# The output gate in one ScalarE function, in a delta-rule attention and mixture-of-experts kernel on one core

## The reference

```
o = scan over time of S = a S + k (v - k S) b;  o_t = q S
o = o * rsqrt(mean(o^2) + eps) * norm_w
o = o * (z * sigmoid(z))             # the gate
out = o @ out_w.T;  x = x + out
...then per token: router, top 2 of 8 experts, relu(x W1) W2, weighted sum
```

## Time and profile before

| | |
|---|---|
| median of 3 runs | 1410.39 us (1410.18 to 1411.52) |
| profiled execution, its own time | 1407.17 us |
| its span | 1405.3 us |
| granted TensorE clock, mean | 0.933 |
| chain that ended last, by engine | DVE 32%, PE 26%, POOL 16%, issue 10%, DMA 7%, ACT 6% |

### The profile page before, as it was taken

One profiled execution on the slowest core, in us unless ns is written; L12 is line 12 of the kernel. 1 busy time (PEld: TensorE's weight loads), 2 busy tenths in 40 slices (PEclk: granted clock), 3 DMA queues, 4 the chain that ended last, 5 costly groups with the idle time before them and its releaser, 6 DMA issues.

```text
span 1405.3 us, 33741 instructions
## 1 busy us (share of the span) xinstructions
PE 1172.5 (83%) x11978; PEld 944.4 (67%) x11978; DVE 1167.0 (83%) x2531; ACT 834.4 (59%) x2536; POOL 710.7 (51%) x598
## 2 busy tenths in 40 slices
PE   0355989898989899898989899999898988469992
PEld 0233868686868686777777777777777777358881
DVE  6878898988888889888888889898989894578875
ACT  1242666665666666666666656566665655348884
POOL 3151726465545555564646373828291914235552
PEclk9996999998989999999999999999999999789996
DMA  6031212222122222222212131313030314332225
GB/s 206 0 98 31 73 36 71 57 59 61 54 62 53 62 54 62 54 61 54 63 52 66 49 69 47 83 35 97 21 99 21 105 18 134 95 105 74 79 64 180
DMA packets 163174, 97.07 MB, mean 69 GB/s; under 512 B 115623, under 2 KB 148269, under 8 KB 161988
## 3 DMA queue, kind: packets, MB, share of 16 engines
q1 hardware_dynamic: 124932, 82.25, 21.5%
q10 hardware_dynamic: 33536, 4.20, 2.1%
q0 software_dynamic: 4544, 8.47, 1.9%
HBM read 73.31 MB, written 24.61 MB: 70 GB/s over the span
## 4 chain that ended last, share of the span: by engine, by line
DVE 32%; PE 26%; POOL 16%; issue 10%; DMA 7%; ACT 6%; SPq 2%; POOLq 0%; DVEq 0%; ACTq 0%
POOL kq L637 9%; DVE Y_sb L1056 7%; DVE blkT L1060 7%; PE kx L1541 3%; POOL decay L629 3%; POOL rows_in L609 2%; DMA blkN<-scr_n 2%; PE kx L1636 2%; POOL kq L620 2%; PE rc L1703 2%; DVE blkN L1047 2%; DVE Gs L1204 1%; DVE area L1146 1%; ACT Gs L836 1%; PE rc L1704 1%
## 5 line engine op out<-in xcount | busy, mean ns | idle before, releaser
L637 POOL TENSOR_TENSOR kq<-tapA,area 128x256 f32<-128x256 f32 x256 | 253.2, 1003 | 89.1 <-DVE area L1146 88.1
L758 ACT ACTIVATE area<-pj,taps 128x256 f32<-128x256 f32 x256 | 123.3, 482 | 138.8 <-PE pj L1555 130.4
L1056 DVE TENSOR_TENSOR Y_sb<-blkT,blkN 128x4 f32<-128x4 f32 (+18 forms) x304 | 172.4, 567 | 10.5
L1541 PE MATMUL kx<-kq 128*128 128x128 f32 x1024 | 143.1, 288 | 43.2 <-ACT area L767 32.6
L609 POOL DMA_INDIRECT rows_in<-rowbuf,dest x64 | 64.8, 1012 | 214.8 <-DVE dest L1132 187.3
L1541 PEld LDWEIGHTS kx<-kq 128*128 128x128 f32 x1024 | 130.2, 199 | 57.8 <-issue 41.2
L1143 DVE SCALAR_TENSOR_TENSOR tapA<-pj,taps,tapA 128x256 f32<-128x256 f32 x256 | 122.2, 477 | 51.7 <-ACT tapA L758 49.8
L620 POOL TENSOR_TENSOR kq<-kq,area 128x1024 f32<-128x1024 f32 x64 | 151.1, 2363 | 0.0
L1060 DVE TENSOR_REDUCE blkT<-Y_sb 128x2 f32<-128x4 f32 (+18 forms) x304 | 142.5, 469 | 5.2
L758 ACT ACTIVATE tapA<-pj,taps 128x256 f32<-128x256 f32 x256 | 123.1, 481 | 0.0
L1146 DVE SCALAR_TENSOR_TENSOR area<-pj,taps,area 128x256 f32<-128x256 f32 x256 | 121.4, 474 | 0.0
(11 more groups left out here) (305 smaller groups left out, 3593.6 us busy)
## 6 DMA issues: line engine op xcount, KB each, us to landing
area<-scr_alpha SPq DMA_DIRECT2D x32, 512.0 KB, 4.2
area<-scr_acum SPq DMA_DIRECT2D x32, 512.0 KB, 3.8
blkN<-scr_n SPq DMA_DIRECT2D x32, 256.0 KB, 4.3
area<-rows_in SPq DMA_DIRECT2D x39, 130.0 KB, 2.2
scr_n<-area SPq DMA_DIRECT2D x128, 32.0 KB, 1.6
area<-rows_out SPq DMA_DIRECT2D x4, 1024.0 KB, 8.0
rows_in<-rows_in SPq DMA_DIRECT2D x8, 260.0 KB, 3.8
kq<-in_x SPq DMA_DIRECT2D x4, 512.0 KB, 6.0
```

What stands on the lines that cost most here:

```text
L637: nc.gpsimd.tensor_tensor(dst[:, n % H, :], tapA[:, n % RING, :], tapB[:, n % RING, :], ALU.add).then_inc(conv_done, 1)
L758: ins = nc.scalar.activation(dst[:, n % RING, :], pj[n % 2][:, k:k + GT], ACT.Copy, scale=taps[:, t, k:k + 1])
L1056: ins = nc.vector.tensor_tensor(p4, bc(blkT[:, r0:, j:].rearrange("p r (o m) -> p r o m", o=1), [128, nr, w, wd]), bc(blkN[:, j:j + w, j:] ...
L1541: ins = mm(o, lhs[:, hh, cs], rhs_[:, hh, cs], start=True, stop=True)
```

## The change

The step `zt` of ScalarE applies Silu instead of Tanh, with scale 1/64 instead of 0.5/64, and raises `zg_ready` itself. The VectorE step `zg` is no longer there (the words `zg.c.u` stay in `ORDER` and issue nothing). ScalarE waits for `g_ready` of the group being finished before it overwrites `zg`. The output weights are scaled by norm_w / 256 only. The semaphore `z_tanh` is gone; the first count of `zg_ready` is given by ScalarE.

```diff
@@ ScalarE, before the first stage
-            for t in (z_tanh, kd_ready, rhs_ready, u_ready, sq_done, gn_ready, gt_ready):
+            for t in (zg_ready, kd_ready, rhs_ready, u_ready, sq_done, gn_ready, gt_ready):
                 act.sem_inc(t, HALVES)
@@ ScalarE, prepare, step "zt"
                         c, u = arg
+                        if g is not None:
+                            act.wait_ge(g_ready, halves(g, c, u))
                         act.wait_ge(z_mm, halves(a, c, u))
-                        nc.scalar.activation(zg[:, c, HU * u:HU * u + HU, :], heads(pj[u]), ACT.Tanh,
-                                             scale=0.5 / WSCALE).then_inc(z_tanh, 1)
+                        nc.scalar.activation(zg[:, c, HU * u:HU * u + HU, :], heads(pj[u]), ACT.Silu,
+                                             scale=1.0 / WSCALE).then_inc(zg_ready, 1)
@@ VectorE, before the first stage
-            nc.vector.tensor_scalar(ow[:, :, :], ow[:, :, :], nw[:, 0:1], 0.5 / WSCALE / VSCALE, ALU.mult,
+            nc.vector.tensor_scalar(ow[:, :, :], ow[:, :, :], nw[:, 0:1], 1.0 / VSCALE, ALU.mult,
                                     ALU.mult).then_inc(s_wsplit, 1)
...
-            for t in (n_ready, at_ready, zg_ready, S_ready, g_ready):
+            for t in (n_ready, at_ready, S_ready, g_ready):
                 dve.sem_inc(t, HALVES)
@@ VectorE, prepare
-                    elif step == "zg":
-
-                        c, u = arg
-                        dve.wait_ge(z_tanh, halves(a, c, u))
-                        nc.vector.scalar_tensor_tensor(out=half(zg, c, u), in0=half(zg, c, u), scalar=1.0,
-                                                       in1=heads(pj[u]), op0=ALU.add, op1=ALU.mult).then_inc(zg_ready, 1)
```

More of the change, by code:

```diff
@@ L197, in preln_delta_moe_kernel @@
         (diag_ready, decay_done, kk_ready, n_ready, ktr_ready, kd_ready, scale_ready, kq_ready, at_ready,
-         ka_ready, aq_ready, z_mm, z_tanh, zg_ready) = sems(
+         ka_ready, aq_ready, z_mm, zg_ready) = sems(
             "diag_ready decay_done kk_ready n_ready ktr_ready kd_ready scale_ready kq_ready at_ready ka_ready "
-            "aq_ready z_mm z_tanh zg_ready")
+            "aq_ready z_mm zg_ready")
         (blk_in, inv_step, inv_done, t_out, t_in, rdiag) = sems("blk_in inv_step inv_done t_out t_in rdiag")
```

## The result

| | before | after |
|---|---|---|
| median of all runs, same chip | 1410.18 us | 1416.12 us |
| lowest and highest of 13 runs | 1405.44, 1413.25 | 1412.64, 1421.15 |
| profiled execution, its span | 1407.17, 1405.3 us | 1415.49, 1413.6 us |
| mean granted clock of TensorE | 0.933 | 0.926 |
| periods of L490, 13 of them from the third tick on | 890.10 us | 893.82 us |

The ratio is 1.0047, 95% interval 1.0031 to 1.0063: the changed kernel is slower by half a per cent. The forecast was 0.7% faster, and 1416 lies above its range.

The account below looks back on a forecast made before the run. No engine full; the stage's chain of waits bounds it, VectorE handing to POOL at the seam. -9.8 (13 stages) - 0.5 (start) + 0.6 (tables) = -9.7 us: profiled 1407.17 to 1397.5, median 1400.5 us, range 1391 to 1410.

Parts of the forecast that it names:

- What bounds the kernel, and the hand-over to POOL: Seam of two stages: VectorE's gate steps stand directly before its hand-over to POOL; the scatter would start 1.19 us earlier.
- 13 stages at 0.75 us: Stages with a scatter: POOL's earlier start would save 0.75 us each, bounds 0 and 1.21; 9.8 us in all.
- The quiet stage: Period before the first scatter, 67.05 us, 1.21 less than the mean of twelve; taken as measure of POOL's lead.
- rival A: Seam of two stages: held by the DRAM round trip alone, so only 0 to 3 us gained, 1409 us; chance 0.17.
- the first pair: Gate steps `zg.0.0`, `zg.0.1` ahead of `ps`: without them the scatter and POOL's head of the next stage start 1.19 us earlier.
- The second pair at nothing: Gate steps behind `ps`, ahead of `at` and `st`: costed at nothing, as ScalarE and the round trip hold the first tap.
- The rule that I had cited as neutral: VectorE instructions with two SBUF inputs and GpSimd's share an exclusive port; removed steps never held POOL, so the sum stays.
- Rival C: TensorE loses its clock at the seam more often, 2.7 us per stage, 1436 us if in all 13; chance 0.06.
- The idle before T64 stays as long: Argument against more clock loss: TensorE loses no work and its idle time before the T64 transfer is unchanged.
- Tables: ScalarE: if Silu needs another table, one hidden load and one before the last Exp; 0 to 1.3 us lost, value 0.6.
- The start: First stage: `z.1.0` no longer waits for VectorE's last `inv` step; 0 to 1.2 us gained, value 0.5.
- the wait on `g_ready`: ScalarE's new wait in `zt`: already met when reached; up to 3.5 us if all on the path, costed at none.

Follow-up runs that it names:

- e2_early_ps: The kernel before with only the destinations step `ps` moved ahead of VectorE's gate steps, so the scatter starts 1.2 us earlier; 0.9982 of the kernel before.
- h1_second_pair: The kernel before with only the second pair of VectorE's gate steps removed, that half made by one ScalarE Tanh step, factor z left out; 0.9998 of the kernel before.
- g2_fill: The changed kernel with four 128x512 filler matmuls on TensorE ahead of the second chunk's wait for T64, results unused; 1.0010 of the kernel before.
- a_fill_pad128: The changed kernel with four filler matmuls ahead of TensorE's wait for T64 and 128 met waits at its queue's head; 1.0018 of the kernel before.
- e1_tanh: The changed kernel with Tanh at the old scale instead of Silu, factor z left out, so no second table loads; 1.0039 of the kernel before.
- h0_first_pair: The kernel before with only the first pair of VectorE's gate steps removed, that half made by one ScalarE Tanh step, factor z left out; 1.0028 of the kernel before.

## Why the prediction was wrong, point by point

*What bounds the kernel, and the hand-over to POOL.* Right in kind: scatter at 1.42 us, scan at 2.3 to 3.0 us, VectorE idle ahead of the first tap, nothing shorter behind the second scan.

*The term "13 stages at 0.75 us".* Mis-sized: 0.29 us in nine ordinary stages of the changed kernel, 0.33 in e2_early_ps, which has that term alone, 4.3 us instead of 9.8. The quiet stage was no experiment for POOL's lead only. It also had no scatter traffic beside the reads of T64, and POOL was 4.9 us ahead, not 1.2. Over the nine ordinary stages the first scan takes 2.73 us on the mean instead of 3.74, a full microsecond less and as forecast, but the second scan starts only 0.38 us earlier behind the tick and the period is 0.29 us shorter: other holders took the rest. In the stage above these are the broadcast of alpha and the first tap, which is where it was; on the mean no run separates them. This much was in the bounds (0 to 1.21), and by itself would have left a gain of 0.2 to 0.3%, which is nearer to rival A (0 to 3 us) than to the forecast.

*The step that failed* is the sentence on the first pair: "Gone, `ps` starts at 743.99 [...] and the scatter starts 1.19 us earlier, and with it POOL's head of the next stage". The start did come 1.2 us earlier; what failed is its price: I priced what the earlier scatter helps and put at nothing what it does to the round trip. The scatter moved into the same four microseconds as the write half of the round trip; there code packets now delay the write in 3 to 5 stages of an execution. Shown are the comparison of the profiles (first pair gone four late writes, second pair gone none, at one placement) and the 42 packets behind one of 16 KB; that it is the scatter's early start in the first pair's going is what the table of kernels suggests, with its cause open. The four stages cost +10.2 us in the profiled execution, more than the whole ordinary gain of 3.8; nearly all of it is in the three that also lost the clock (70.10, 72.00, 71.68 us), two of them with a held scan. I had named the round trip as the next bound, and costed its length as given (3.65 to 3.71 us in every stage of before) where it was the thing that could grow.

*The second pair at nothing.* Right: h1_second_pair, 0.9998. TensorE does start its projections earlier (`proj.0` 2.88 instead of 2.96 us, `v.0.0` 3.55 instead of 3.92), and gains nothing, as said.

*The same lead with the other sign.* In 10 of 30 stages with a late write POOL's lead holds the scan up instead of letting it go: 5.53 us in the stage shown, against the 4.57 that was the worst before. The rule that I had cited as neutral (the exclusive port of the Trainium skill, "SBUF — State Buffer", section "SBUF: two separate sides") was the one that turned the lead into a loss; the trace agrees with it here, the scan ending 2.14 us behind POOL's last piece.

*Rival C, the clock,* was the nearest: it gave 0.06 to "TensorE loses its clock at the seam more often", decided "from the fourth such stage". Its price held: a stage with the clock lost is 2.9 us longer (70.97 against 68.09) where 2.7 was said. Under the change low clocks came in 1 to 4 middle stages, before in 1 to 3, so they are no clear sign of the change alone; but they come more often with a late write (12 of 30 against 11 of 87), and all three long stages of the changed kernel have one. g2_fill and a_fill_pad128, which remove all of them and most late writes, give back 0.37 and 0.50%. How that splits between clock and write stays open, because the filler shifts TensorE's queue and with it the packets. "The idle before T64 stays as long" was wrong where the write is late.

*The small parts.* Tables +1.28 us at the end and nothing in the stages, as costed. The Trainium skill, "ScalarE: Activation LUTs", section "What ACT_TABLE_LOAD costs", puts a switch at about 2.66 us, of which about 1.28 are the load and the rest a drain. The trace has the load and not the drain: at 1312.24 ScalarE's step before ends 0.02 us ahead of the load, and its Exp starts 0.02 us behind it. e1_tanh without the loads stands at 1.0039 against 1.0047, no difference that can be told. The start and the wait on `g_ready`: nothing that can be seen. *Behind the last tick* +3.9 us had no term in the sum but the table's 1.28. The rest goes together with the 6.8 us at 1.2 GHz in the last stage, but that the change made these is not shown: where such a stretch lies in the last stage differs from kernel to kernel, without a pattern that I could tie to the change, and e2_early_ps has it at the same place.

*The chances.* 0.13 for slower was too low. I had counted mechanisms of the kernel's own list only, and none that depends on what else is on the 16 DMA engines.

## What to carry to other kernels

A round trip through DRAM in small packets, on the path once per stage, is over only with its last packet, and where a code packet came in among them it was 0.5 to 1.8 us longer; before an edit moves other work or its transfers towards such a stretch, look at the instruction queues in the window, in several stages, and not only at its median length. A stage that got longer has more than one cause to look for: read the granted clock and the scan beside the late transfer before giving the whole loss to it. Give a lead to one engine only together with the question what it holds when its partner is late. And when one engine's work can go early by reordering alone, as here `ps` ahead of `zg.0.0` (0.9982), try that first: it took the gain and mostly kept the loss away, while the edit that also removed 38 us of VectorE's time was slower.

## What the runs showed of the hardware

- TensorE's code arrives during the run, 100 packets of 16,384 bytes in 1414 us on queue 8, each 0.9 to 1.5 us long, beside the data: in h0_first_pair 42 of 1040 packets of a write start only when one code packet is nearly through. Waits that are met and do nothing still take room in it: 128 of them at the head of the queue brought its first packet 3.4 us forward (53.0 to 49.6) and moved the kernel before by 0.35% and the changed one by 0.2%.
- The scan over 128x1024 takes 2.28 us alone and up to 5.75 us among POOL's instructions (32 scans of the changed kernel: shortest 2277, median 2281, longest 5755 ns).
- 8 us ahead of T64 with 6.66 us busy were followed by a granted clock of 0.79, and 8 us with 7.41 busy by 1.00; but 7.75 busy in a third stage were followed by 0.79 too, so the busy share alone doesn't tell it. With four matmuls in that stretch that compute nothing TensorE had no 1.2 GHz from 4 to 50 us behind the tick in any middle stage, at two placements.
- Silu runs from the same table set as Copy, Square and Relu here (one load of 1.28 us ahead of the first Silu, the next at 1312.24, behind 16 stages and the first Relus), and Exp from another.
